# First layer's gather in three one-pass terms, and shorter score rings: one change to a four-layer graph kernel

## What is computed

```python
# layer 0
e2 = (adj @ h) * (diag + 1.0)
x  = x + (h - e2) @ weight + bias
# layer 2, twice
Wh, Ws = split(h @ W[l])
a = softmax(Wh @ Ws.T) * adj
h = leaky_relu(a @ Wh + h, 0.01)
# layer 3, in each of its two steps
logits = (Xa @ W1) @ W2 @ (Xa @ W3).T
A  = softmax of logits, cut to the smallest set of entries with mass 0.9
Xa = A @ Xa
# layer 3 also needs the row sums and the column sums of adj
```

## Time and profile before

| | |
|---|---|
| median of 3 runs | 1182.63 us (1181.18 to 1183.73) |
| profiled execution | 1182.82 us, its span 1181.0 us |
| TensorE matmuls, weight loads | 948.8 us (80%), 782.4 us (66%) |
| VectorE, ScalarE, GpSimd | 756.2 us (64%), 512.4 us (43%), 37.6 us (3%) |
| mean granted TensorE clock | 0.913 of full speed |

### The profile page before, as it was taken

The page is one execution under the profiler, slowest core; times in us unless marked ns, Lnnn a source line. Parts: engine busy times, 40 slices in busy tenths (PEclk is TensorE's granted clock), DMA queues, the critical chain, the costliest instruction groups (busy, mean ns, idle before and its releaser), DMA issues.

```text
span 1181.0 us, 14131 instructions
## 1 busy us (share of the span) xinstructions
PE 948.8 (80%) x4873; PEld 782.4 (66%) x4873; DVE 756.2 (64%) x1288; ACT 512.4 (43%) x886; POOL 37.6 (3%) x101
## 2 busy tenths in 40 slices
PE   4998899957999779996789498979798047966883
PEld 3788788856899778996668347867543024555773
DVE  4653455453566436774479993323599999996994
ACT  4104744264233332334568814423588851022332
POOL 0000000000010000000130000000100000000000
PEclk9999999978999899997999798989989569996997
DMA  9000000000000000001114200001112001000001
GB/s 344 19 1 1 21 1 1 1 1 1 1 0 0 19 1 1 1 0 47 50 49 138 84 0 1 1 18 45 41 49 73 1 0 50 0 1 1 1 0 48
DMA packets 42896, 32.69 MB, mean 28 GB/s; under 512 B 3218, under 2 KB 40796, under 8 KB 42844
## 3 DMA queue, kind: packets, MB, share of 16 engines
q1 hardware_dynamic: 42844, 32.02, 8.7%
HBM read 30.63 MB, written 1.39 MB: 27 GB/s over the span
## 4 chain that ended last, share of the span: by engine, by line
DVE 17%; PE 17%; issue 13%; ACT 6%; ACTq 0%; DVEq 0%; POOL 0%
PE out L791 6%; ACT u_rows_a L590 4%; DVE run L1386 3%; PE scores L822 2%; DVE e_strip L1502 2%; PE scores L907 2%; DVE tmp L1377 2%; DVE small L1285 2%; DVE is_tie L1455 1%; DVE e_strip L1506 1%; DVE kept_tile L1377 1%; PE turned_ps L925 1%; PE scores L832 1%; PE turned_ps L832 1%; PE scores L701 1%
## 5 line engine op out<-in xcount | busy, mean ns | idle before, releaser
L590 ACT ACTIVATE u_rows_a<-e_rows,small 128x1354 f32<-128x1354 f32 x104 | 146.6, 1411 | 20.1 <-DVE small L1324 20.1
L762 PE MATMUL out<-feat,adj_t 128*128 128x256 f32 (+1 forms) x484 | 109.2, 384 | 1.5 <-DVE x_rows L1100 1.5
L791 PE MATMUL out<-h_rows,adj_strip 128*128 128x256 f32 x484 | 109.5, 383 | 0.0
L762 PEld LDWEIGHTS out<-feat,adj_t 128*128 128x128 f32 x484 | 92.6, 192 | 16.1 <-DVE x_rows L1100 1.9
L791 PEld LDWEIGHTS out<-h_rows,adj_strip 128*128 128x128 f32 x484 | 91.9, 193 | 11.9
L907 PE MATMUL scores<-feat_fb,adj_strip 128*128 128x512 f32 x154 | 73.5, 636 | 18.6 <-ACT feat_fb L615 15.1
L484 ACT ACTIVATE y_rows<-scores,small 128x1354 f32<-128x1354 f32 x22 | 30.7, 1393 | 128.9 <-DVE small L1237 128.9
L1330 DVE SCALAR_TENSOR_TENSOR tmp<-e_rows,small 128x1354 f32<-128x1354 f32 x52 | 84.5, 1625 | 0.0
L691 PE MATMUL turned_ps<-ident,tmp 128*128 128x128 f32 x132 | 30.6, 329 | 55.4 <-ACT tmp L425 38.3
L907 PEld LDWEIGHTS scores<-feat_fb,adj_strip 128*128 128x128 f32 x154 | 31.5, 207 | 57.9 <-issue 38.6
L1237 DVE TENSOR_REDUCE small<-scores 128x1354 f32 (+1 forms) x22 | 34.5, 1569 | 45.7 <-PE scores L802 45.7
(11 more groups left out here) (330 smaller groups left out, 2214.0 us busy)
## 6 DMA issues: line engine op xcount, KB each, us to landing
adj_strip<-in_adjT SPq DMA_DIRECT2D x22, 704.0 KB, 4.7
adj_t<-in_adjT SPq DMA_DIRECT2D x11, 704.0 KB, 13.0
u_weights<-in_L_gnn_U SPq DMA_DIRECT2D x8, 256.0 KB, 5.2
x_rows<-in_x SPq DMA_DIRECT2D x2, 512.0 KB, 4.1
tmp<-in_L_gnn_W_stack SPq DMA_DIRECT2D x2, 512.0 KB, 4.4
out_rows<-y_rows SPq DMA_DIRECT2D x2, 512.0 KB
tmp<-in_L_gnn_U SPq DMA_DIRECT2D x2, 256.0 KB, 2.9
x_rows<-in_x SPq DMA_DIRECT2D x1, 384.0 KB, 6.5
```

The source lines that it names most:

```text
L590: act.activation(out2[:, (k % 2) * N:(k % 2 + 1) * N], E[:, t, :], [ACT.Relu, ACT.Sign][k % 2], bias=nudged[:, t:t + 1], accum_out=[relu_s ...
L762: ins = pe.matmul(bank[:, 0:n], AT[:, j, cols(t)], features[:, j, 0:n], start=(j == 0), stop=(j == NT - 1))
L791: ins = pe.matmul(OUT[b][:, 0:D], ADJ[:, b, j, :], H[:, j, :], start=(j == 0), stop=(j == NT - 1))
```

## The change

**Layer 0.** The projection writes `feat_hi` and `feat_lo` instead of `feat1`, which puts a third VectorE operation into each evacuation. The gather becomes the three-term `gather` that layer 2 uses: 33 one-pass matmuls per tile. Its strips are made from `adj_t`: ScalarE copies the high part and then a row of `adj_t` once more, with an accumulator that yields the column sum (VectorE's sums go away); VectorE subtracts for the rest. Strip t+2 takes the buffer of tile t, so it is made once tile t is gathered. The first strip goes to the buffer that the projection leaves free (`swap`).

**Layer 2.** Scores alternate between the two PSUM tiles, and a tile's exponentials are turned back into the tile from which its scores came. Scores of tile t now wait for the mask of tile t-2.

**Layer 3.** The 64 idle rows are used: query high and low parts lie one above the other in `AQ`, the key columns are there twice, and two matmuls per chunk, by the high and by the low part of the keys, give all four products. GpSimd's copies become two of 64 partitions.

```diff
+            AQ = sb("aq_hi_lo", [P, 2, P], F32R, scope)
+                    pool.tensor_copy(AQ[0:64, b:b + 1, :], TQH[0:64, 0:1, cols(t)])
+                    pool.tensor_copy(AQ[64:P, b:b + 1, :], TQL[64:P, 0:1, cols(t)]).then_inc(q_staged, 1)
...
+            def strip_l0(t, b):
+                wait(act, gathered, GA["L0"] + t - 1)
+                act.activation(SH[:, 1 - b, :, :], AT[:, :, cols(t)], ACT.Copy).then_inc(strip_hi, 1)
+                if not isinstance(t, int) or t >= 1:
+                    act.wait_ge(col_sums, t)
+                act.activation(expt[0], AT[:, bass.ds(t, 1), :], ACT.Copy,
+                               accum_out=colsum[:, bass.ds(t, 1)]).then_inc(col_sums, 1)
+            def first_strip_l0(t, r):
+                if isinstance(t, int) and t == NT - 1:
+                    act.wait_ge(ld_adj, 16 * NT)
+                    strip_l0(0, 0)
...
+                         before=[(3, first_strip_l0)])
             act.wait_ge(projected, PJ["L0"] + NT)
+            strip_l0(1, 1)
             split_w("L1", WH[:, :, 0:D + 6 + D], raw[:, :, 0:D + 6 + D])
...
+            for t in range(2, NT):
+                strip_l0(t, t % 2)
...
-            pipeline(pe, (0, gather_l0), peel=NT)
+            pipeline(pe, (0, gather("L0", one, swap=True)))
...
             def evac_l0(t, r):
+                lo(row(FL, t), pbank[b][0][:, D:2 * D], row(FH, t))
...
+            def strip_rest_l0(t, b):
+                wait(dve, strip_hi, STR["L0"] + t + 1)
+                wait(dve, gathered, GA["L0"] + t - 1)
+                lo(SL[:, 1 - b, :, :], AT[:, :, cols(t)], SH[:, 1 - b, :, :]).then_inc(strip_lo, 1)
...
-            pipeline(dve, (0, sum_column), (0, read(GA["L0"], read_l0)))
+            for t in range(NT):
+                if t + 2 < NT:
+                    strip_rest_l0(t + 2, t % 2)
+                read_tile_l0(t, t % 2)
...
-                    wait(pe, exped, s0 + t)
+                    wait(pe, masked, m0 + t - 1)
...
-                                ins = pe.matmul(SC[:, c:c + n], q[:, b, k, :], k2[:, KB + k, c:c + n],
+                                ins = pe.matmul([SC, TP][b][:, c:c + n], q[:, b, k, :], k2[:, KB + k, c:c + n],
...
-                        ins = pe.transpose(TP[:, j * P:(j + 1) * P], expt[b][:, j * P:(j + 1) * P], ident[:, :])
+                        ins = pe.transpose([SC, TP][b][:, j * P:(j + 1) * P], expt[b][:, j * P:(j + 1) * P], ident[:, :])
...
-                        for m, (q, k2) in enumerate([(AQH, TQH), (AQL, TQH), (AQH, TQL)]):
-                            ins = pe.matmul([SC, TP][b][:, c:c + n], q[:, b, :], k2[:, 1, c:c + n], start=(m == 0),
-                                            stop=(m == 2))
+                        pe.matmul([SC, TP][b][:, c:c + n], AQ[:, b, :], TQH[:, 1, c:c + n], start=True, stop=False)
+                        ins = pe.matmul([SC, TP][b][:, c:c + n], AQ[:, b, :], TQL[:, 1, c:c + n], start=False,
+                                        stop=True)
...
-            dve.memset(raw[:, :, 64:128], 0.0)
-            dve.memset(raw[:, :, 192:256], 0.0).then_inc(raw_ready, 1)
+            dve.tensor_copy(raw[:, :, 64:128], W12[:, :, :])
+            dve.tensor_copy(raw[:, :, 192:256], raw[:, :, 128:192]).then_inc(raw_ready, 1)
```

More of the change, by code:

```diff
@@ L40 @@
 GA = {name: NT * k for k, name in enumerate(["L0", "L1b", "L1a", "L2a", "L2b", "A0", "A1"])}
-STR = {name: NT * k for k, name in enumerate(["L2a", "L2b", "A0", "A1"])}
+STR = {name: NT * k for k, name in enumerate(["L0", "L2a", "L2b", "A0", "A1"])}
 GAL1A = [GA["L1b"] + 2 * t + 2 for t in range(NT)]
@@ L743, in project_rows, with gather, step @@
                 pipeline(pe, (1, turn(p0)), (3, project(p0, body)), peel=peel, ring=RT)
-            def gather(name, *groups):
-                def step(t, b):
+            def gather(name, *groups, swap=False):
+                def step(t, place):
+                    b = 1 - place if swap else place
                     wait(pe, strip_hi, STR[name] + t + 1)
@@ L753, in step @@
                             for j in range(NT):
[L754 removed]
+                                ins = pe.matmul(OUT[place][:, c0:c0 + n], left[:, b, j, :], right[:, j, 0:n],
                                                 start=(m == 0 and j == 0), stop=(m == 2 and j == NT - 1))
@@ L894, in _ @@
                 pe.wait_ge(proj_hi, PJ[name] + NT)
-                pipeline(pe, (0, scores_l2(SCO[name])), (1, turn_l2(SCO[name], MSK[name])), (2, gather(name, one)))
+                pipeline(pe, (0, scores_l2(SCO[name], MSK[name])), (1, turn_l2(SCO[name])), (2, gather(name, one)))
             def gather_s(t):
@@ L1098, in evac_l0, with first_rest_l0 @@
                 b = r % 2
+                lo(row(FL, t), pbank[b][0][:, D:2 * D], row(FH, t))
                 link0(t, 1, dve.tensor_tensor(row(X, t), row(X, t), pbank[b][0][:, 0:D], ALU.add))
                 return dve.tensor_tensor(row(X, t), row(X, t), bcast[:, :], ALU.add)
-            project_rows(PJ["L0"], evac_l0)
+            def strip_rest_l0(t, b):
+                wait(dve, strip_hi, STR["L0"] + t + 1)
+                wait(dve, gathered, GA["L0"] + t - 1)
+                lo(SL[:, 1 - b, :, :], AT[:, :, cols(t)], SH[:, 1 - b, :, :]).then_inc(strip_lo, 1)
+            def first_rest_l0(t, r):
+                if isinstance(t, int) and t == NT - 1:
+                    dve.wait_ge(ld_adj, 16 * NT)
+                    strip_rest_l0(0, 0)
+            pipeline(dve, (2, turn(PJ["L0"])), (3, first_rest_l0), (4, evac(PJ["L0"], evac_l0)), peel=7, ring=RT)
+            strip_rest_l0(1, 1)
             dve.wait_ge(proj_read, PJ["L0"] + NT)
@@ L1119, in read_l0 @@
                 return stat(t, X)
-            def sum_column(t, b):
-                dve.tensor_reduce(one(colsum, t), AT[:, bass.ds(t, 1), :], AX.X, ALU.add).then_inc(col_sums, 1)
-            dve.wait_ge(ld_adj, 16 * NT)
-            pipeline(dve, (0, sum_column), (0, read(GA["L0"], read_l0)))
+            read_tile_l0 = read(GA["L0"], read_l0)
+            for t in range(NT):
+                if t + 2 < NT:
+                    strip_rest_l0(t + 2, t % 2)
+                read_tile_l0(t, t % 2)
             dve.wait_ge(gather_read, GA["L0"] + NT)
@@ L1236, in top @@
                     wait(dve, scored, SCO[name] + t + 1)
-                    dve.tensor_reduce(one(nmax, t), SC[:, 0:N], AX.X, ALU.max, negate=True).then_inc(maxed, 1)
+                    dve.tensor_reduce(one(nmax, t), [SC, TP][b][:, 0:N], AX.X, ALU.max, negate=True).then_inc(maxed, 1)
                 def mask(t, b):
@@ L1242, in mask @@
                     wait(dve, strip_lo, STR[name] + t)
-                    dve.tensor_tensor(strip, TPS, AT[:, :, cols(t)], ALU.mult).then_inc(masked, 1)
+                    dve.tensor_tensor(strip, turned_a[b], AT[:, :, cols(t)], ALU.mult).then_inc(masked, 1)
                 def lo_masked(t, b):
```

23 lines of the change are left out of this document (11 added, 12 removed).

## The result

| | before | changed |
|---|---|---|
| median | 1183.06 us | 1165.26 us (4 runs, 1163.39 to 1166.81) |
| ratio, 95% interval | | 0.9851 (0.9829 to 0.9874) |
| the profile's span | 1181.0 us | 1164.8 us |
| mean granted clock | 0.913 | 0.909 |

The change saves 17.6 us (14.9 to 20.2), where the sum said 25.1. The time lies inside the range, 7 us above the likeliest value. The two traces tell where these 7 us are.

A forecast was written before the change was run, and what follows sets the result against it. TensorE was taken to bound the layer-0 gather and layer-2 loop, a latency circle layer 3. Gains of 6.1 + 6.4 + 5.4 + 7.3 - 0.1 = 25.1 us from 1182.82 gave 1158 us, range 1151 to 1169.

The forecast's parts named there:

- several of the low bounds at once, 1164 to 1170: Whole kernel: several low-end estimates of the gains hold together, ending at 1164 to 1170 us; chance 0.08.
- main case: Whole kernel: the forecast with its bounds, up to 1164 us; chance 0.80.
- Layer-0 gather, tile length: Layer-0 gather: 33 one-pass matmuls at 119 ns make a tile 3.94 us, where it took 4.79.
- the upper bound of 8 us: Layer-0 gather: it ends 8 us earlier, in place of 6.1, if the tiles come out shorter.
- What must hide: Layer-0 gather: ScalarE's 2.98 and VectorE's 2.63 us a tile hide; the strip chain of 4.1 us gives a 4.02 us period.
- the slower rival: Layer-0 gather: ScalarE's high part and column sum set the tile period; at 7.5 us the kernel takes some 1195; chance 0.03.
- Its start: Layer-0 gather: starts 1.5 us later; the third evacuation operation on VectorE costs nothing, at most 3.8 us if cover fails.
- The clock at the start: Layer-0 gather: low clock after TensorE's 2.9 us idle costs 0 to 1.7 us, taken as 0; the next stall is 1.1 us.
- Layer-2 starts: Start of each layer-2 pass: second scores follow the first at once, saving 6.4 us in the first pass, 5.4 in the second.
- The bound for the clock, 1.7 us: Layer-2 starts: if the remaining idle time of 1.7 to 1.9 us halves the clock, 1.7 us go back per pass.
- Layer-3 scores: Layer-3 score loops: six matmuls in place of nine cut the circle from 5.61 to 5.00 us, saving 7.3 us for both layers.
- the first rival: Layer-3 loops: the clock falls, the circle is 6.2 us and the 7.3 us become a loss, up to 1172 us; chance 0.05.

The follow-up runs named there:

- the experiment on the strip chain: Changed kernel with VectorE reading tile t before making the rest of strip t+2, and layer 1's weight work spread behind the reads: ratio 0.9835.
- the layer-0 part: Kernel before with only the change's layer-0 edits, layers 2 and 3 as before: ratio 0.9989, a gain of 1.3 us.

## Why the prediction was right, and where it was off

The mechanism was right within each of the three parts (shorter tiles, second scores at once, a shorter circle), and so was the sign. The size was off by 7 us, of which layer 0 has 4.8: little of what its gather gained reached the end. The measured time lies where the prediction put 0.08 ("several of the low bounds at once, 1164 to 1170"), not in the 0.80 of its main case. The largest loss was none of those that its range was made for, so that the total still fell inside is partly luck.

*Layer-0 gather, tile length:* right, 3.94 us where nothing waits (the experiment on the strip chain). The 109 ns that the prediction quotes from the Trainium skill (TensorE: Matmul & The Clock Gate, section Back-to-back issue gap) are given there for an isolated matmul, without the weight load that each matmul has here. The runs show 119 ns, and none shows the shorter tiles that the upper bound of 8 us counts on.

*What must hide:* right about ScalarE (1.38 + 1.37 + 0.18 us, not the bound, so the slower rival falls) and about the chain, but "0.1 for hand-offs" was 0.25: tile 3 ends at 56.44 + 3.94 = 60.38, tile 5 starts at 64.63, 4.25 us later. 0.6 us over the gather.

*Its start:* "I cost at nothing during the projection" failed. A projected tile waits for the evacuation two tiles back, so VectorE's third operation is in a round of waits, and a busy share of 68% is no cover for it: 1.4 us at the first strip, of which 1.0 is left at the start of the gather (42.74 against 41.7).

*The clock at the start:* "I take 0, since the next wait absorbs most of it" was half right. The slow first tile cost 1.6 us, and the stall of 1.1 us absorbed 0.9 of it. Start, clock and hand-offs together, 1.0 + 0.7 + 0.6 = 2.3 us, are nearly all that the gather's end missed (3.6 us in place of 6.1).

*What has no term in the sum:* the gain was carried past layer 1 as if an earlier start were an earlier end. There the second gather, which others wait for, ran at the low clock: some 3 us of the 4.3 were lost in the layer-0 part, and 2.2 us (by the medians) to 3.2 us (by the means) came back when the idle time ahead of it was filled. This is the largest single error, and the experiments show it twice. That the change itself brings this about is not shown: it came in all six profiles that have the layer-0 part and no added matmuls in layer 1, but also in two of five with layer 0 as before, one of them with 18 added matmuls.

*Layer-2 starts:* right: 4.7 to 6.3 us against 6.4, and 5.3 against 5.4; 10.9 against 11.8 by the runs. The bound for the clock, 1.7 us, is what the third scores of the first pass lose when they fall into it.

*Layer-3 scores:* right in the circle (5.00 us), too high by 1.3 us in the runs. A sign of being wrong that the prediction named did come, a clock below 0.95 in these loops: 0.82 and 0.90. So the first rival happened in part, with the clock at 0.50 over one or two rounds of each loop and not throughout; on the chain that ends last this cost 1.9 us in the first loop (26.7 against 24.8) and next to nothing in the second. The Trainium skill (TensorE: Matmul & The Clock Gate, section A second HAM failure mode: psum-queue depth-cycling) says that the clock can swing in such a loop; the trace agrees, with 0.50 at 587.3 and at 829.5. The columns that the change removed had kept TensorE at work: with them back, off the circle, no low stretch is left behind the first round.

## What to carry to other kernels

Count a gain only where the next wait ends: an earlier start is followed through the stages behind it, and the granted clock is read there, because work behind a wait may run at the low clock and take back what was won. Read a new operation's cover from the round of waits it stands in, not from its engine's busy share. Idle times of 2 to 4 us in front of work that others wait for can be filled with matmuls that nobody reads, if they reach nearly to the end of the wait: 30 that left 0.80 us did it here, 18 that left 2.24 us did not. Such fillings, the added matmuls of layer 3 and a turned order were worth 9.5 us together, after the change itself had given 18.

## What the runs showed of the hardware

The same code, after the same idle times (1.24 and 0.5 us ahead of the first gather of layer 1), ran once partly at the low and once at the full clock: 6.77 us at 0.75 and 5.10 us at 1.00. What decides it is open: with the layer-0 part it was the second gather that ran slowly in every profile taken without added matmuls there, with layer 0 as before it was sometimes the one and sometimes the other. An idle time of 2.70 us cost nothing in the one trace and one of 2.19 us cost 1.6 us in the other, so the length of an idle time alone does not tell.
